# One first stage for constants, normalisation and projections, the context loaded and projected batch by batch

## The reference, cut to what matters

```python
xn   = (x - mean(x)) / sqrt(var(x) + 1e-5)          # 896 x 512
q_c  = xn @ W_dq                                    # 512 -> 192, padded to 256
kv_c = ctx @ W_kvc                                  # 512 -> 128, for 8 x 375 keys
k_r  = rope(kv_c @ W_kr)                            # kv_c @ W_kr times cos, plus the swapped one times sin
good = (k_ids <= seg_id) & (k_ids >= seg_id - 8)    # the mask, 112 x 375 for each batch
# of layer 2, done early because it needs nothing but the context:
ctx_sums[d, b] = sum_t coef[t] * ctx[b, t, d]       # coef[t]: sums of powers of sigmoid(decay)
```

## Time and profile before

| | |
|---|---|
| median of 3 runs | 2459.88 us (2458.32 to 2461.79) |
| the profiled execution | 2462.96 us, of which span 2461.2 us |
| start to the first matmul of the attention | 72.3 us |
| of it: set-up, to DVE's first instruction on `x` | 11.4 us |
| of it: normalisation, to the first matmul on `xnT` | 11.0 us |
| of it: projections and masks, to the first matmul of the attention | 49.9 us |

### The profile page before, as it was taken

The page is one execution under the profiler, slowest core; times in us unless marked ns, Lnnn a source line. Parts: engine busy times, 40 slices in busy tenths (PEclk is TensorE's granted clock), DMA queues, the critical chain, the costliest instruction groups (busy, mean ns, idle before and its releaser), DMA issues. The chain is left out here.

```text
span 2461.2 us, 33504 instructions
## 1 busy us (share of the span) xinstructions
PE 2288.3 (93%) x9625; PEld 1368.7 (56%) x9626; DVE 983.1 (40%) x2522; ACT 714.1 (29%) x1673; POOL 372.7 (15%) x513
## 2 busy tenths in 40 slices
PE   7899999998888899998999999699999999799898
PEld 4444444444565566666456554355655655356587
DVE  5645455444333433335612223771222222602375
ACT  2445353530111466666011110211111111051221
POOL 6100000000112100000011114301111111600061
PEclk9999999998999999999999999799999999999999
DMA  9401010022865100001446655042444542561220
GB/s 345 125 1 35 0 35 0 0 94 70 262 220 162 31 10 14 14 14 37 144 150 204 204 182 172 22 161 94 151 150 133 167 161 75 163 233 39 89 90 30
DMA packets 169969, 263.72 MB, mean 107 GB/s; under 512 B 13134, under 2 KB 106702, under 8 KB 169373
## 3 DMA queue, kind: packets, MB, share of 16 engines
q1 hardware_dynamic: 139869, 186.06, 23.0%
q0 software_dynamic: 15040, 49.30, 6.7%
q10 hardware_dynamic: 14976, 27.27, 2.9%
HBM read 212.78 MB, written 49.81 MB: 107 GB/s over the span
## 5 line engine op out<-in xcount | busy, mean ns | idle before, releaser
L1207 PE MATMUL bank<-f2r_wd,f2b_hT 128*128 (+1 forms) x300 | 137.2, 593 | 1.4 <-DVE f2b_hT L1311 1.4
L1188 PE MATMUL bank<-f2r_wg,f2b_xT 128*128 x400 | 129.2, 467 | 1.9 <-issue 1.9
L1188 PE MATMUL bank<-f2r_wu,f2b_xT 128*128 x400 | 126.8, 460 | 0.0
L1298 DVE TENSOR_TENSOR f2b_h<-bank,f2b_acted 128x352 f32<-128x352 f32 x50 | 26.2, 525 | 202.9 <-PE bank L1188 202.9
L1645 PE MATMUL bank<-l0a_vo,l0a_zT 128*128 128x512 f32 x224 | 101.5, 596 | 3.2 <-DVE l0a_zT L1810 3.2
L1188 PEld LDWEIGHTS bank<-f2r_wu,f2b_xT 128*128 128x128 f32 x400 | 76.3, 191 | 42.8 <-issue 0.7
L1709 ACT ACTIVATE l0a_p<-l0a_p,l0a_low 112x375 f32<-112x375 f32 x128 | 77.2, 607 | 77.5 <-DVE l0a_low L1801 76.4
L1791 DVE CUSTOM_DVE_ANT_0 l0a_p<-bank,xn 112x375 f32<-112x375 f32 x128 | 70.3, 549 | 67.5 <-PE bank L1617 35.7
L1615 PE MATMUL bank<-l_kvcT,xnT 128*112 128x375 f32 x256 | 92.3, 482 | 5.0 <-ACT xnT L1738 5.0
L1986 PEld LDWEIGHTS bank<-l1w_v,ctxT 128*125 128x125 f32 x768 | 88.7, 188 | 8.4 <-issue 0.6
L1188 PEld LDWEIGHTS bank<-f2r_wg,f2b_xT 128*128 128x128 f32 x400 | 73.1, 193 | 35.0 <-issue 3.9
(11 more groups left out here) (409 smaller groups left out, 4291.7 us busy)
## 6 DMA issues: line engine op xcount, KB each, us to landing
slot_rows<-zeros SPq DMA_DIRECT2D x2, 7424.0 KB, 38.3
slot_rows<-f2b_y ACTq DMA_DIRECT2D x50, 256.0 KB, 3.5
f1r_wg<-in_l_wg SPq DMA_DIRECT2D x16, 704.0 KB, 4.2
f1r_wu<-in_l_wu SPq DMA_DIRECT2D x16, 704.0 KB, 5.6
f2r_wg<-in_l_wg SPq DMA_DIRECT2D x16, 704.0 KB, 4.3
f2r_wu<-in_l_wu SPq DMA_DIRECT2D x16, 704.0 KB, 5.6
xn<-in_l_w_ffn SPq DMA_DIRECT2D x11, 768.0 KB, 4.4
l_raw<-in_l_w_ffn SPq DMA_DIRECT2D x11, 768.0 KB, 4.4
```

What stands on the lines that cost most here:

```text
L1188: mm = pe.matmul(bank[:, 0:width], xT[:, v, k, :], w[:, bass.ds(at, 1), k, :].rearrange("p o f -> p (o f)"), start=(k == 0), stop=(k == KD ...
L1207: mm = pe.matmul(bank_y[v][:, :], hT[0:fn, v, c, :], wd[0:fn, bass.ds(at, 1), c, :].rearrange("p o f -> p (o f)"), start=(c == 0), stop=(c ...
```

## The change

The three stages become one Block, `first_stage`, with no barrier inside it. `make_constants` is the old list of POOL, word for word; the old `setup_stage` and `layernorm_stage` go.

- **Loads.** SP issues `decay`, `w_kvc`, then the context by batches (8 DMAs of 750 KB, rows of 1500 bytes, where there were 4 of 1500 KB with rows of 12000) mixed with `x` in four parts: context 0, 1, x tiles 0-1, 2-3, context 2, x tiles 4-5, 6, context 3, `w_dq`, the other tables, context 4 to 7, gates, the attention's weights, the clearing of scratch.
- **PE.** It projects context 0 and 1, transposes x tiles 0 and 1, projects context 2, transposes 2 and 3, projects context 3, transposes 4 to 6; then the four query pieces; then for each batch the rope products and transposes, and behind each of the first four the projection of one more batch (4 to 7).
- **Weighted sums.** For batches 4 to 7 DVE takes them as before (`sum`). For batches 0 to 3 POOL makes the products (`weigh`, one multiply of 128x1500) and ACT adds them up (`add_up`, four copies with an accumulator). There are two buffers for products, so `weigh` of batch 2 waits for `add_up` of batch 0, and `weigh` of batch 3 for `add_up` of batch 1.
- **Masks.** POOL makes them behind the constants, the four `weigh` and a wait for the last transpose of `xn`.

The core of the diff:

```diff
-    def sum(self, dve, share, shares):
+    def weigh(self, pool, b):
         s = self.s
-        for i in range(share * KD * B // shares, (share + 1) * KD * B // shares):
...
+        pool.wait_ge(self.coef_made, 1)
+        if b >= 2:
+            pool.wait_ge(self.added, KD * (b - 1))
+        pool.tensor_tensor(self.products[:, b % 2, :, :], s.ctxT[:, :, b * T:(b + 1) * T],
+                           self.coef[:, :].unsqueeze(1).to_broadcast([128, KD, T]), ALU.mult).then_inc(self.weighed, 1)
+
+    def add_up(self, act, b):
+        s = self.s
+        act.wait_ge(self.weighed, b + 1)
+        for k in range(KD):
+            act.activation(self.products[:, b % 2, k, :], self.products[:, b % 2, k, :], ACT.Copy,
+                           accum_out=s.ctx_sums[:, k, b:b + 1]).then_inc(self.added, 1)
...
+def first_stage(nc, s, d, a, w):
+    EARLY = 4
+    x_parts = (slice(0, 2), slice(2, 4), slice(4, 6), slice(6, 7))
...
             sums.load(sp, d)
+            w.load_kvc(sp, d)
+            load_context(0)
+            load_context(1)
+            load_x(0)
+            load_x(1)
+            load_context(2)
+            load_x(2)
+            load_x(3)
+            load_context(3)
+            w.load_dq(sp, d)
+            w.load_others(sp, d, a)
+            for b in range(EARLY, B):
+                load_context(b)
...
             a.load_weights(sp, d, 0)
+            sp.wait_ge(consts, 5)
             clear_scratch(sp, s)
...
         @block.gpsimd
         def _(pool):
-            pool.wait_ge(loaded, 112)
+            make_constants(pool, s, iota_i, made, consts)
+            for b in range(EARLY):
+                pool.wait_ge(ctx_loaded[b], 16)
+                sums.weigh(pool, b)
+            pool.wait_ge(w.loaded, 16 * 5)
             pool.tensor_copy(ids[:, :], ids_i[:, :]).then_inc(ids_f, 1)
             pool.wait_ge(ids_f, 1)
+            pool.wait_ge(turned, TILES)
             for b in range(B):
...
+        @block.tensor
+        def _(pe):
...
+            pe.wait_ge(w.kvc_loaded, 16)
+            project_context(0)
+            project_context(1)
+            pe.wait_ge(made, 4)
+            turn_x(0)
+            turn_x(1)
+            project_context(2)
+            turn_x(2)
+            turn_x(3)
+            project_context(3)
+            turn_x(4)
+            turn_x(5)
+            turn_x(6)
+            pe.wait_ge(w.dq_loaded, 16)
+            for q in range(4):
+                project_query(q)
+            pe.wait_ge(w.loaded, 16 * 5)
+            pe.wait_ge(q_copied, 4)
+            for c in range(B):
+                rotate_and_turn(c)
+                if EARLY + c < B:
+                    project_context(EARLY + c)
...
+            for n in range(4, TILES):
+                copy_x(n)
+            for q in range(4):
+                act.wait_ge(q_done, q + 1)
...
+            for c in range(B):
+                copy_turned(c)
+                if EARLY + c < B:
+                    copy_context(EARLY + c)
+                    sums.add_up(act, c)
+            act.wait_ge(g_loaded, 32)
+            act.activation(s.tanh_g[:, :], s.raw_g[:, :], ACT.Tanh)
...
+                if c < B - EARLY:
+                    dve.wait_ge(ctx_loaded[EARLY + c], 16)
+                    sums.sum(dve, EARLY + c)
```

More of the change, by code:

```diff
@@ L147, in clear_semaphores @@
         self.nc.all_engine_barrier()
[L150 to L209, removed]
@@ L222, in logits_of @@
     return s.bank[6][0:P, 0:TILES * E].rearrange("p (b e) -> p b e", b=TILES)
[L225 to L271, removed]
-                for k in range(KD):
-                    mm = pe.transpose(s.bank[n % 4][:, k * P:(k + 1) * P],
-                                      s.xn[:, n, k * 128:(k + 1) * 128], s.ident[0:P, 0:P])
-                mm.then_inc(tr_done, 1)
@@ L1367, in __init__ @@
         self.s = s
-        self.loaded, self.exp_done, self.step, self.summed = s.sems("l2s", "loaded", "exp_done", "step", "summed")
+        self.loaded, self.exp_done, self.step, self.summed, self.coef_made, self.weighed, self.added = s.sems(
+            "l2s", "loaded", "exp_done", "step", "summed", "coef_made", "weighed", "added")
+        self.count = 0
         self.decay = sb("decay", [128, 1])
@@ L1375, in __init__ @@
         self.weighted = sb("weighted", [128, 2, T])
+        self.products = sb("products", [128, 2, KD, T])
     def load(self, sp, d):
@@ L1518, in _ @@
-        @block.vector
-        def _(dve):
-            sums.coefficients(dve)
-            dve.wait_ge(s.ctx_loaded, 16 * KD)
-            for b in range(B):
-                sums.sum(dve, b, B)
-                dve.wait_ge(rot_done, b + 1)
-                if b >= 2:
-                    dve.wait_ge(rot_added, b - 1)
-                for v, table in enumerate((a.cos, w.sin)):
-                    dve.tensor_tensor(part[:, b % 2, v, :], s.bank[2 + 2 * (b % 2) + v][:, 0:T], table[:, :],
-                                      ALU.mult).then_inc(rot_mul, 1)
-                dve.wait_ge(rot_mul, 2 * (b + 1))
-                dve.tensor_tensor(a.krT[:, b * T:(b + 1) * T], part[:, b % 2, 0, :], part[:, b % 2, 1, :],
-                                  ALU.add).then_inc(rot_added, 1)
@@ L2768, in build @@
                     w = ProjectWeights(nc, of_projections, s)
-                    setup_stage(nc, s, d, beside=lambda sp: w.load(sp, d, a))
-                    layernorm_stage(nc, s, "ln0")
-                    latent_project_stage(nc, s, d, a, w)
+                    first_stage(nc, s, d, a, w)
                 latent_attention_stage(nc, s, d, a)
-        else:
-            setup_stage(nc, s, d)
         if 1 in parts:
```

247 lines of the change are left out of this document (174 added, 73 removed).

## The result

The changed kernel takes **2484.53 us** in the median of 4 runs (2478.01 to 2486.44), beside 2460.16 us (2458.32 to 2461.79, 4 runs) for the kernel before: a ratio of **1.0102**, 95% interval 1.009 to 1.0115. It is slower by 24.4 us. The profiled execution took 2484.85 us. Its page's first line stands first, then the busy time by stretch, with the columns of the earlier trace rows: the queries, the part behind them up to DVE's last work, and what is left up to the attention.

A forecast was written before the change was run, and what follows sets the result against it. The first stage was taken as bound by POOL's masks, delayed by products waiting for ACT; the attention would start at 94.2 us, not 72.3. So 2459.88 + 21.9 = 2482 us, range 2476 to 2493.

The forecast's parts named there:

- queries start: First stage on PE: queries start at about 23.6 us, where they started at 22.44; bounds 22.4 and 28.
- masks: POOL, end of first stage: masks start at 51.8 us, take 41.6 us and end at 93.4.
- The sum: First stage, step by step to the attention's start: 94.2 us instead of 72.3, 21.9 us later.
- The loads set its pace: Front, up to the queries: loads at 334 GB/s decide, context 3 landing at 18.4 us.
- half the clock: Rival, PE's front: a projection takes 5.0 us, queries 10 us back, 2492 us; 6 in 100.
- counter-evidence: Against the half-clock rival: the program's first weight loads, 0.71 / 4 = 0.18 us, were taken as full speed.
- DVE's 63 us: Behind the queries: PE done at 59.3 us, DVE 4 us later at 63; alone, attention 8.4 us earlier.
- At no cost: First stage: POOL's constants, `tanh` at ACT's end and SP's later scratch clearing were said to cost nothing.
- POOL isn't held up: Rival, POOL: masks start at about 23.6 us, time 2452 to 2457 us, faster than before; 5 in 100.
- turning point of some 30 us: POOL: masks that start before some 30 us leave the stage no longer than it was.
- PE released by DVE at the barrier: Sign in the profile at the attention's start, meant to show the decisive step wrong.
- the decisive step: POOL: late products wait for ACT's `add_up`, so masks start 29 us later and end the stage.

The follow-up runs named there:

- e1_four_buffers: The changed kernel with four product buffers instead of two, so no product waits for ACT; 2460.35 us, ratio to before 1.0004.
- e3_roots_first: The changed kernel with ACT's first two roots ahead of its copies of context 0 and 1; one run, 2481.18 us.
- e7_warm: The changed kernel with 20 transposes of the identity added on PE ahead of the first context projection; one run, 2490.95 us.
- e8_all_warm: e6_all with 20 transposes of the identity added on PE ahead of context 0; 2451.55 us, 0.9971 of before.
- e4_sums_on_dve: The changed kernel with the sums of batches 0 to 3 on DVE too, no products on POOL; 2458.81 us, ratio to before 1.0003.
- e2_half_masks: The changed kernel with the masks of batches 0 to 3 only; one run, 2459.19 us.
- e5_early_masks: e4_sums_on_dve with the masks in a buffer of their own and the ids loaded early; 2448.38 us, ratio to before 0.9962.
- e6_all: e5_early_masks with ACT's roots of x tiles 0 and 1 ahead of its copies of context 0 and 1; 2449.1 us, ratio to before 0.9968.

## Why the prediction was right, and where it was not

Sign, size and mechanism were as forecast: POOL's masks end last, because two products ahead of them wait for ACT's adding up. (POOL waited 33.2 us there and not some 20, since its first two products were done at 14.03 us; that moves nothing.) Step by step, in us:

| step | forecast | measured |
|---|---|---|
| queries start | 23.6 | 27.29 |
| ACT's first `add_up` starts | 41.2 | 45.00 |
| third product | 44.1 to 47.5 | 47.26 to 50.18 |
| fourth product | 48.2 to 51.6 | 51.37 to 54.76 |
| masks | 51.8 to 93.4 | 55.33 to 96.64 |
| attention starts | 94.2 | 97.50 |
| DVE ends | 63 | 70.34 |

- **The sum was 3.3 us short, and the first line alone is 3.7.** From the queries on, each step came within some tenths and 0.4 us were won back: the masks took 41.3 us (41.6 forecast, 4.97 us each when alone), a product 2.9 to 3.4 us (3.34), the barrier 0.86 us (0.83). ACT's four sums were quicker, 2.1 us against 2.9: its rows come every 0.50 us here, not 0.72 as in the earlier trace rows.
- **"The loads set its pace" was wrong.** Context 3 was to land at 18.4 us, and in `e1_four_buffers`, with the same loads, its landing released POOL at 18.98. But PE reached it only at 21.63 us: 3.2 of the 3.7 us were lost ahead of it, in steps for which the sum had no term. One is shown: the order in which ACT copies and takes roots (`e3_roots_first`: 1.4 us). The rest is argued and overlaps: `x` tiles 0 and 1 landed at 11.39 us, 1.5 later than the sum's 9.9, so DVE started no sooner than before; ACT's table load of 1.28 us stands ahead of the first root; and PE's first two projections took 8.23 us, and 5.28 in `e7_warm`. Had context 2 in `e7_warm` taken 2.69 us, as in the kernel after, 1.7 us more could have been gained there, and that isn't shown either. The near hit on context 3 has luck in it: from 8 to 14 us the DMAs moved 378 GB/s, not 334, and still the first tiles of `x` came late.
- **The rival "half the clock" came in part, and its counter-evidence was misread.** The earlier trace rows took 0.71 us for four weight loads as proof of full speed. Those were loads for transposes, and they can't be laid beside a matmul's 0.34: four loads for transposes take 0.42 us in `e7_warm` at 14.42 us, before its clock fell. So 0.71 was the lower level, as in `e8_all_warm`, where four such loads took 0.71 us at 16.98 us, just ahead of its slow projection. From PE's weight loads in the two:

```profile
14.42 0.42 PEld L1482 LDWEIGHTS bank<-ident,xn 128*128 128x128 f32 x4 [1.81 <-issue]
...
16.98 0.71 PEld L1479 LDWEIGHTS bank<-ident,xn 128*128 128x128 f32 x4 [1.24 <-DVE xn L1599]
```

  Also the granted-clock column shows 1.00 for the stretch from 8 to 14 us of the kernel after, in which a weight load takes 0.34 us, as it does at a granted 0.50 in `e7_warm`: so at the start of this kernel the durations tell the level and the column doesn't. It cost no 10 us, as the rival priced it, but at most the 2.95 us by which contexts 0 and 1 were slower than in `e7_warm`, since context 2 and 3 took 2.69 us each at a granted clock of 1.00.
- **DVE's 63 us were missed by 7.3, at no cost.** The prediction let POOL's product be slowed by DVE, but not DVE by the product. Both late products hold a sum of DVE for their whole length (0.54 us is its usual time):

```profile
47.38 3.19 DVE L1350 CUSTOM_DVE_ANT_0 l2s_weighted<-ctxT,l2s_coef 128x375 f32<-128x375 f32 x1
...
51.45 3.73 DVE L1350 CUSTOM_DVE_ANT_0 l2s_weighted<-ctxT,l2s_coef 128x375 f32<-128x375 f32 x1
```

  They end at 50.57 and 55.18 us, each 0.4 us behind the product's end. The two holds are 5.8 us more than two usual sums, and the queries were 3.7 us late; together that is more than the 7.3, so some of it fell into waiting that was there anyway. A further 1.10 us is DVE's wait for PE's last rope products, four instructions that took 2.62 us at a granted clock of 0.50 (66.1 to 68.5 us), not 1.42. Without the products DVE ended at 64.11 us (`e4_sums_on_dve`), so the 63 was a fair figure for a DVE that isn't held. PE, which waits for DVE to free its banks, ended at 69.05 us instead of 59.3.
- **"At no cost" held only under cover.** `tanh` and its table load at ACT's end cost nothing while POOL ended 25 us later. With the masks out of the way they were the stage's last work, 0.76 us behind DVE, and the prediction had put no price on that.
- **The rival "POOL isn't held up" was priced too well.** `e1_four_buffers` is that case, and it gave no gain: the masks began at 29.95 us, not 23.6, because the products held DVE's normalising and the front was late already. That is the rival's own turning point of some 30 us, and there it came out: the attention started 1.2 us later than before.
- **One sign was badly chosen.** "PE released by DVE at the barrier" was to mean that the decisive step was wrong, and the trace does name DVE there. It is the sign that fails, not the step: DVE was done 26 us before POOL, and `e2_half_masks` shows that POOL was last.
- **That the profiled span came out at the forecast's 2483 is partly luck**: 3.3 us too little in the first stage, and 3.3 us less in the stages behind it, which scatter. The medians give +24.4 us, nearer to the +25.2 of the first stage.

## What to carry to other kernels

Work moved ahead of a queue's last consumer makes that consumer wait for everything that the moved work waits for (here 33.2 us, POOL's wait for ACT): before handing an idle engine something new, follow each buffer that it reuses to the instruction that frees it, and count where that one stands in its own engine's list. When stages are merged, ask of each engine not how much less it does but when its longest uninterrupted piece (here 41 to 45 us of masks) can start, since that piece ends the stage. And the gain of such a change may be real and hidden; it came out (0.4%) when the buffer shared with `xn` and the products on POOL were given up.

## What the hardware showed that was not expected

- A DVE sum with two inputs or a normalising that started beside a POOL instruction with two inputs ended 0.3 to 0.4 us behind it: sums beside a product took 3.19 and 3.73 us instead of 0.54 (the kernel after), normalisings of 512 columns beside a product 2.76 and 2.60 instead of 0.55 (`e1_four_buffers`), and one beside a mask's sum of 0.98 us took 1.06 (`e5_early_masks`). Beside the mask's steps with one input the traces show both. In `e4_sums_on_dve` a first step runs from 26.23 to 28.58 us, a sum that starts at 26.66 within it takes its usual 0.54 and the next one 0.83, and it is the step that stretches, from 1.56 to 2.35; but a sum that starts at 32.24 beside a fourth step, which runs from 31.99 to 32.69 us, takes 0.85 and ends 0.40 us behind it. The statistics of a tile, 0.69 us at 11.39 in the middle of a product of the kernel after, weren't held at all.
- Extra work to raise TensorE's clock gained 0.24 us in one kernel and lost 1.85 us in the other: PE, then ahead of its supplier, had gaps of 1.24 and 0.73 us in the one and 1.91 and 1.00 in the other, and took 4.37 and 3.87 us for the next context instead of 2.69. In the kernel after, where PE started slowly and had gaps of 0.22 and 0.73 us, that projection took 2.69 us at a granted clock of 1.00. The gaps go with it without extra work too: 1.11 and 0.73 us ahead of 4.38 in `e5_early_masks`, 2.80 and 0.73 ahead of 3.72 in `e1_four_buffers`, but 0.59 and 0.73 ahead of 2.69 in `e4_sums_on_dve`, and one of 0.97 ahead of 2.69 in `e6_all`.
